# Layer 0's causal triangle as a 128-column matmul instead of GpSimd's selects

## The chip, the cores and the metric

The kernel runs on one core of a Trainium2 chip. The core has TensorE (PE, matmuls into PSUM), VectorE (DVE), ScalarE (ACT), GpSimd (POOL) and SyncE (SP, which issues most DMAs). The metric is the device time of one execution in microseconds, as the median of several runs.

## The reference, cut to what matters

Two pre-norm transformer layers follow one another: attention and a mixture of experts, then attention and a feed-forward with 4-bit weights. The change lies in the attention of layer 0, with 4 batches, 512 tokens, 16 heads of width 16 and a causal mask:

```
b, s, d = x.shape                                # 4, 512, 256
qkv = jnp.einsum('bsd,od->bso', x, w_project)    # reshaped to 3 x 16 heads x 16
att = jnp.einsum('bhqd,bhkd->bhqk', q, k) / math.sqrt(HEAD_DIM)
causal = jnp.triu(jnp.ones((s, s), dtype=bool), k=1)
att = jnp.where(causal[None, None, :, :], jnp.float32(-1000000000.0), att)
att = jax.nn.softmax(att, axis=-1)
out = jnp.einsum('bhqk,bhkd->bhqd', att, v)
...
x = x + _L0_attn_ref(_layernorm(x, axis=-1), L0_attn_w_project, L0_attn_w_out)
```

## The kernel before

Layer 0's attention takes a batch at a time (4 batches; the middle two are turns of a hardware loop), and in a batch four groups of four heads (`g` 0 to 3), so 16 groups in all. Each engine has its own program, written out by hand, and the engines meet at semaphores. One list (`in_group`) sets the order of a group's steps on PE, ACT and DVE alike.

A group has six **score units** (`ST_UNITS`, `score_unit`, line 661 on PE). A unit computes transposed scores, keys on partitions and queries on columns, for the key block `kt` (128 keys) and the queries from that block on. Units 0 and 1 are two heads each with 512 columns (`kt` 0), units 2 and 3 two heads each with 384 columns (`kt` 1), unit 4 four heads with 256 columns (`kt` 2), unit 5 four heads with 128 columns (`kt` 3). The row maximum has been folded into the matmul's rows, so that ACT can take the exponential right away (`exponentials`, line 766) and write `pt` in SBUF. The first 128 columns of each head are the diagonal block, in which half of the entries are to be zero. GpSimd zeroes them in `pt` with one select for each unit (line 530), and counts the semaphore `masked`. PE's **values** (`values`, line 675, four steps `kt` 0 to 3) multiply `pt` by `v`, and wait for `masked`. The scores lie in two pairs of PSUM banks, so unit u waits until ACT has read unit u-2.

Between these steps the list puts **work** for the next group or batch, in two further PSUM banks: the row maxima (`max_scores`, lines 582 and 586 on PE, reduced by DVE on line 857, ten items for each group), the turning of the maxima (line 609; DVE writes them as `mt_hi` and `mt_lo`, and SP copies these into the rows of `qs`), and in group 0 of each batch also the values of the batch (line 547), the transposed input of the next batch (lines 554, 725, 815), its queries and keys (lines 547, 730, 820), and the projection of the batch before (lines 594, 602, 853). A work item waits until DVE has read the item two places before. `max_scores` masks its own diagonal blocks already by a second matmul with `maskneg` (-3e38 above the diagonal) and the identity, accumulated onto the block (line 586). That is the pattern that the change uses.

GpSimd has other work in this stage: nine pieces for each batch (`split_next`, lines 482 to 499), which split a quarter of the next stage's weights after the DMA `w_next` has landed. Its program takes them between the selects: in batches 0 to 2 from group 1 on, behind every second unit; in the last batch behind every unit of groups 0 and 1.

Of the kernel before, what the change touches and what calls it, by code (L numbers as in the profile page):

```python
# [21 lines left out]
ALU = mybir.AluOpType  # L22
# [3 lines left out]
P = 128  # L26
# [22 lines left out]
def reach(eng, sem, value):  # L49

    if not (isinstance(value, int) and value <= 0):
        eng.wait_ge(sem, value)


def wait_alone(eng, sem, value, passed):

    eng.wait_ge(sem, value)
    eng.sem_inc(passed, 1)
# [3 lines left out]
def work_between(pieces):  # L62

    todo = iter(pieces)

    def some(k=1):
        for piece in islice(todo, k):
            piece()
    return some
# [100 lines left out]
def tie_break(e):  # L170

    return (4 - e) * STEP
# [88 lines left out]
def layer0_attention(nc, glob, A):  # L261
    X, ps, ident, identb = glob["X"], glob["ps"], glob["ident"], glob["identb"]
    passed_dve, passed_pool, passed_sp = glob["passed"]
    scratch_q, scratch_k = glob["scratch_q"], glob["scratch_k"]
    with ExitStack() as stack:
        st = Store(nc, stack)
# [8 lines left out]
        maskneg = st.sb("maskneg", [P, P], BF16)  # L275
# [11 lines left out]
        qs = st.sb("qs", [SHIFT + 2, H0, S], BF16)  # L287
        ks = st.sb("ks", [SHIFT + 2, H0, S], BF16)
# [5 lines left out]
        pt = [st.sb(f"pt{k}", [P, HG, S - P * k], F32) for k in range(G)]  # L294
# [26 lines left out]

        s_work, s_taken, s_mx = st.sem("bank_work"), st.sem("bank_taken"), st.sem("row_max")
        s_mthi, s_shift = st.sem("mthi"), st.sem("shift")
        s_st, s_exp, s_msk, s_pv = st.sem("scoreT"), st.sem("expd"), st.sem("masked"), st.sem("pv0")
        s_raw, s_den, s_rec, s_oT = st.sem("raw0"), st.sem("den0"), st.sem("rec0s"), st.sem("oT0")
        s_norm = st.sem("norm0")
        s_xr, s_xrlo, s_mag0, s_lg0, s_ties = (st.sem(n) for n in ("xr0", "xrlo0", "mag0", "lg0s", "ties_made"))
# [9 lines left out]
        ST_UNITS = [(0, (0, 1)), (0, (2, 3)), (1, (0, 1)), (1, (2, 3)), (2, (0, 1, 2, 3)), (3, (0, 1, 2, 3))]  # L337
# [18 lines left out]
        def all_batches(eng, batch):  # L356
            batch(0, True, False)
            with eng.Fori(1, B - 1) as b:
                batch(b, False, False)
            batch(B - 1, False, True)  # L360
# [11 lines left out]
        with nc.Block() as block:  # L372
# [86 lines left out]
            @block.gpsimd  # L459
            def _(pool):  # L460
                pool.memset(ones_row[:, :], 1.0).then_inc(const, 1)
                pool.memset(half[:, :], -0.5).then_inc(const, 1)
                pool.memset(maskneg[:, :], 0.0).then_inc(const, 1)

                pool.wait_ge(const, 3)

                pool.affine_select(out=maskneg[:, :], in_=maskneg[:, :], compare_op=ALU.is_ge, fill=NEG, base=0,
                                   pattern=[[-1, P]], channel_multiplier=1).then_inc(const, 1)

                def split_next(b):  # L470

                    def after(n, ins):
                        def piece():
                            if n is not None:
                                wait_alone(pool, s_next, NEXT * b + n, passed_pool)
                            ins().then_inc(s_next, 1)
                        return piece
                    r_hi, r_lo, e_hi, e_lo = (q[:, b] for q in quarters)

                    def first():  # L480
                        wait_alone(pool, load_next, 32 * b + 32, passed_pool)
                        pool.tensor_copy(r_hi, w_next[:, 0, :, :]).then_inc(s_next, 1)

                    def first_bias():
                        wait_alone(pool, load_b, 32 * b + 32, passed_pool)

                        if not (isinstance(b, int) and b == 0):
                            wait_alone(pool, s_b3, 96 * b, passed_pool)
                        pool.tensor_copy(b_part[:, 0, :], b_next[:, :]).then_inc(s_next, 1)
                    return [  # L490
                        first,
                        after(None, lambda: pool.tensor_copy(e_hi, w_next[:, 1, :, :])),
                        first_bias,
                        after(1, lambda: pool.tensor_tensor(r_lo, w_next[:, 0, :, :], r_hi.bitcast(F32), ALU.subtract)),
                        after(2, lambda: pool.tensor_tensor(e_lo, w_next[:, 1, :, :], e_hi, ALU.subtract)),
                        after(3, lambda: pool.tensor_tensor(b_next[:, :], b_next[:, :], b_part[:, 0, :], ALU.subtract)),
                        after(6, lambda: pool.tensor_copy(b_part[:, 1, :], b_next[:, :])),
                        after(7, lambda: pool.tensor_tensor(b_next[:, :], b_next[:, :], b_part[:, 1, :], ALU.subtract)),
                        after(8, lambda: pool.tensor_copy(b_part[:, 2, :], b_next[:, :])),
                    ]  # L500

                def root(b):

                    wait_alone(pool, s_mv, G * b + G, passed_pool)
                    pool.tensor_scalar(rstd[:, :], mv[:, :, 1], EPS, None, ALU.add).then_inc(s_rstd, 1)
                    wait_alone(pool, s_rstd, 2 * b + 1, passed_pool)
                    pool.tensor_tensor(rstd[:, :], rstd[:, :], half[:, :], ALU.pow).then_inc(s_rstd, 1)

                root(0)
                pool.wait_ge(s_rstd, 2)  # L510
                pool.memset(ones4[:, :], 0.0).then_inc(s_ties, 1)
                pool.wait_ge(s_ties, 1)
                pool.memset(ones4[0:4, :], 1.0).then_inc(s_ties, 1)
                pool.memset(glob["stage"][:, :, :], 0.0).then_inc(rows_set, 1)
                pool.wait_ge(rows_set, 1)
                for e in range(E):
                    pool.memset(glob["stage"][0:4, 0, D * e:D * (e + 1)], -e * ZERO_STEP).then_inc(rows_set, 1)

                def batch(b, first, last):
                    more = work_between(split_next(b))  # L520
                    root(b + 1)
                    if first:
                        for e in range(E):
                            pool.tensor_scalar(ties[:, e, :], identb[:, :], tie_break(e), None, ALU.mult).then_inc(s_ties, 1)
                    for g in range(NG):
                        for u, (kt, heads) in enumerate(ST_UNITS):

                            wait_alone(pool, s_exp, 6 * (NG * b + g) + u + 1, passed_pool)
                            t = pt[kt][:, heads[0]:heads[-1] + 1, 0:P]
                            pool.affine_select(out=t, in_=t, compare_op=ALU.is_ge, fill=0.0, base=0,  # L530
                                               pattern=[[0, len(heads)], [1, P]],
                                               channel_multiplier=-1).then_inc(s_msk, 1)
                            if last and g < 2 or g and u % 2:
                                more()

                all_batches(pool, batch)

            @block.tensor
            def _(pe):
# [111 lines left out]
                def score_unit(b, g, u):  # L651
                    kt, heads = ST_UNITS[u]
                    t = NG * b + g
                    if u == 0:
                        pe.wait_ge(s_shift, 32 * t + 32)

                    reach(pe, s_exp, 6 * t + u - 1)
                    for i, h in enumerate(heads):
                        c, w = st_col(u, i)
                        h += HG * g  # L660
                        mm = pe.matmul(ps[:, c:c + w], ks[:, h, P * kt:P * (kt + 1)], qs[:, h, P * kt:],  # L661
                                       start=True, stop=True, skip_group_check=True)
                    mm.then_inc(s_st, 1)

                def values(b, g, kt, values_taken):
                    t = NG * b + g
                    pe.wait_ge(s_msk, 6 * t + (2, 4, 5, 6)[kt])
                    if kt == 0:

                        reach(pe, s_raw, t)  # L670
                        if g == 0:

                            pe.wait_ge(s_taken, values_taken)
                    for h in range(HG):
                        mm = pe.matmul(ps[HB * h:HB * (h + 1), PVB * BANK + P * kt:(PVB + 1) * BANK],
                                       v[:, kt, HG * g + h, :], pt[kt][:, h, :],
                                       start=(kt == 0), stop=(kt == G - 1), skip_group_check=True)
                    mm.then_inc(s_pv, 1)
# [1397 lines left out]
def build(nc, A, out, phases=(1, 2, 3, 4)):  # L2076
    with ExitStack() as stack:
# [33 lines left out]
        if 1 in phases:  # L2111
            layer0_attention(nc, glob, A)
# [66 lines left out]
```

## Time and profile before

| what | value |
|---|---|
| time, median of 3 runs | 1227.91 us (1227.71 to 1230.26) |
| the profiled execution's own time | 1230.62 us |
| its span | 1228.9 us |
| TensorE busy | 1027.0 us, 84% |
| VectorE, ScalarE, GpSimd busy | 868.6, 499.1, 297.4 us |
| line 530 (GpSimd's selects) | 96 of them, 46.1 us |
| line 661 (score matmuls) | 256 of them |
| layer 0's attention on PE | score units from 49.99 us on, the last values at 286.50 us |

Busy times of different engines overlap, and their sum means nothing. A timeline row gives the start, the length, the engine, the line and the operation; xN says that N instructions of one kind are merged into it; the bracket names the idle time before the first of them and who ended it. A matmul's length holds its way through the array, so the cost of one in a row of several is the distance from its start to the next start. PEclk is the granted clock of TensorE as a share of full speed.

### The profile page before, as it was taken

How to read it: one execution, taken by the hardware profiler on the slowest of the kernel's cores; microseconds unless marked ns; L12 is line 12 of the kernel's file. 1: busy time of each engine (PE TensorE's matmuls, PEld its weight loads, DVE VectorE, ACT ScalarE, POOL GpSimd, SP SyncE). 2: the span in 40 equal slices, each digit the busy share in tenths (PEclk: the TensorE clock that was granted, in tenths of full speed). 3: DMA queues.
4: the chain of work that ended last, by engine and by line, in shares of the span. 5: the costliest groups of instructions: out<-in, count | busy, mean ns of one | idle time of the engine just before them, and what ended most of it. 6: DMA issues, size and time to landing. Idle time of an engine off the chain costs nothing. (4 is left out here: it accounts for less than half of the span.)

```text
span 1228.9 us, 20311 instructions
## 1 busy us (share of the span) xinstructions
PE 1027.0 (84%) x6960; PEld 591.5 (48%) x6960; DVE 868.6 (71%) x1556; ACT 499.1 (41%) x972; POOL 297.4 (24%) x337
## 2 busy tenths in 40 slices
PE   3798888798778788788398898988968799999997
PEld 1344444445444454443144474654746355656564
DVE  4677666643999999999867628448382577777775
ACT  2144444354465564655344314223130244444443
POOL 3233334440423324323111302203143410000000
PEclk9699999898899898897698898898968899999999
DMA  6622121201001010010000100000010100000000
GB/s 168 107 71 87 53 88 52 70 2 43 1 1 43 1 43 0 0 44 0 5 14 10 27 2 18 19 1 26 9 31 22 35 1 18 1 18 0 1 17 18
DMA packets 37082, 35.79 MB, mean 29 GB/s; under 512 B 8584, under 2 KB 33416, under 8 KB 37008
## 3 DMA queue, kind: packets, MB, share of 16 engines
q1 hardware_dynamic: 35728, 33.79, 9.6%
q10 hardware_dynamic: 1280, 1.05, 0.7%
q8 instruction: 42, 0.69, 0.2%
q14 instruction: 32, 0.26, 0.1%
HBM read 27.28 MB, written 6.29 MB: 27 GB/s over the span
## 5 line engine op out<-in xcount | busy, mean ns | idle before, releaser
L857 DVE TENSOR_REDUCE bm<-ps 128x4 f32<-128x512 f32 x160 | 106.3, 685 | 42.0 <-PE ps L586 31.9
L766 ACT ACTIVATE pt<-ps 128x1024 f32<-128x1024 f32 (+1 forms) x96 | 82.7, 881 | 84.3 <-PE ps L661 83.0
L1968 ACT ACTIVATE g<-ps 128x512 f32<-128x512 f32 x64 | 38.2, 597 | 133.0 <-PE ps L1917 133.0
L582 PE MATMUL ps<-ks,qs 96*128 96x512 bf16 (+3 forms) x256 | 71.6, 326 | 23.3 <-DVE bm L857 10.0
L2018 DVE SCALAR_TENSOR_TENSOR g<-g,ps 128x512 f32<-128x512 f32 x64 | 43.9, 685 | 62.6 <-ACT g L1968 62.3
L1726 DVE TENSOR_TENSOR qk_lo<-ps,qk_hi 128x512 bf16<-128x512 f32 x80 | 54.8, 684 | 42.9 <-ACT qk_hi L1618 36.5
L1495 PE MATMUL ps<-xT_hi,wq_hi 128*128 128x512 bf16 x160 | 68.6, 429 | 15.8 <-DVEq L1757 8.8
L155 POOL TENSOR_TENSOR mag_gu<-stage 128x512 f32<-128x512 fp8e4 x20 | 22.0, 1099 | 238.3 <-DVE stage L142 238.3
L1618 ACT ACTIVATE qk_hi<-ps 128x512 bf16<-128x512 f32 x80 | 47.8, 598 | 74.5 <-PE ps L1495 74.4
L1495 PE MATMUL ps<-wp_hi,oT_hi 128*128 128x256 bf16 x256 | 71.2, 278 | 4.9 <-DVE oT_lo L1719 4.9
L530 POOL TENSOR_SCALAR_AFFINE_SELECT pt<-pt 128x256 f32<-128x256 f32 (+1 forms) x96 | 46.1, 483 | 118.7 <-ACT pt L766 118.3
L1932 PE MATMUL ps<-ew_hi,it_hi 128*128 128x256 bf16 x256 | 69.8, 273 | 5.4 <-DVE it_lo L2034 5.4
L1495 PE MATMUL ps<-wp_lo,oT_hi 128*128 128x256 bf16 x256 | 71.0, 277 | 0.0
L1495 PE MATMUL ps<-wp_hi,oT_lo 128*128 128x256 bf16 x256 | 71.0, 277 | 0.0
L1932 PE MATMUL ps<-ew_lo,it_hi 128*128 128x256 bf16 x256 | 69.8, 273 | 0.0
L1932 PE MATMUL ps<-ew_hi,it_lo 128*128 128x256 bf16 x256 | 69.8, 273 | 0.0
L176 PE MATMUL ps<-stage,ones 128*128 128x512 bf16 x128 | 52.2, 408 | 20.3 <-DVE X L1287 8.2
L1495 PE MATMUL ps<-xT_lo,wq_hi 128*128 128x512 bf16 x160 | 68.0, 425 | 0.0
L1167 ACT ACTIVATE far<-far 128x256 f32<-128x256 f32 x128 | 51.3, 402 | 40.4 <-DVE far L1277 40.4
L1287 DVE SCALAR_TENSOR_TENSOR X<-ps,cw,X 128x256 f32<-128x256 f32 (+1 forms) x128 | 61.9, 483 | 8.2 <-DVE X L1287 4.9
L1495 PE MATMUL ps<-xT_hi,wq_lo 128*128 128x512 bf16 x160 | 67.0, 419 | 0.0
L1161 ACT ACTIVATE wt<-wt 128x2048 f32<-128x2048 f32 x16 | 30.6, 1915 | 87.6 <-POOL wt L1026 87.6
(254 smaller groups left out, 2816.1 us busy)
## 6 DMA issues: line engine op xcount, KB each, us to landing
qs<-scratch_q SPq DMA_DIRECT2D x64, 64.0 KB, 2.6
ks<-scratch_k SPq DMA_DIRECT2D x48, 64.0 KB, 2.5
q_next<-in_w_qkv SPq DMA_DIRECT2D x4, 768.0 KB, 4.6
X<-in_x SPq DMA_DIRECT2D x4, 512.0 KB, 7.0
w_next<-in_router_w SPq DMA_DIRECT2D x4, 512.0 KB, 4.1
w_next<-in_expert_w SPq DMA_DIRECT2D x4, 512.0 KB, 5.0
p_next<-in_w_proj SPq DMA_DIRECT2D x4, 512.0 KB, 5.5
out<-X SPq DMA_DIRECT2D x8, 256.0 KB, 2.3
```

The lines of the kernel that those rows point to most:

```text
L176: pe.matmul(out, ones4[:, :], bias, start=True, stop=False)
L530: pool.affine_select(out=t, in_=t, compare_op=ALU.is_ge, fill=0.0, base=0, pattern=[[0, len(heads)], [1, P]], channel_multiplier=-1).then_ ...
L582: pe.matmul(ps[:, o + P * i:o + P * (i + w)], qs[0:SHIFT, h, P * j:P * (j + 1)], ks[0:SHIFT, h, P * k0:P * (k0 + w)], start=(i == 0), stop ...
L766: act.activation(pt[kt][:, heads[0]:heads[-1] + 1, :], src, ACT.Exp).then_inc(s_exp, 1)
L857: ins = dve.tensor_reduce(bm[:, 2 * g + i // 5, 4 * (i % 5):4 * (i % 5) + 4], src.rearrange("p (k q) -> p k q", k=4), AX_X, ALU.max)
L1167: act.activation(far[:, e, :], far[:, e, :], ACT.Copy, accum_out=cw[t % 2][:, e:e + 1]).then_inc(s_cw, 1)
L1287: dve.scalar_tensor_tensor(x, bank(4 + u, D, D * e), c_t[:, 2 * u + e:2 * u + e + 1], x, ALU.mult, ALU.add).then_inc(s_c, 1)
L1495: mm = pe.matmul(out, lhs[a](c), rhs[b_](c), start=(n == 0), stop=(n == 3 * chunks - 1), **kw)
L1618: act.activation(qk_hi[:, m // (HQ + 1), m % (HQ + 1), :], bank(QK_BANK[m]), ACT.Copy).then_inc(s_qkhi, 1)
L1726: dve.tensor_tensor(qk_lo[:, k, h, :], bank(QK_BANK[m]), qk_hi[:, k, h, :], ALU.subtract).then_inc(s_qklo, 1)
L1932: mm = pe.matmul(bank(6 + t // 2, D, D * (t % 2)), a[m % 2][:, P * t:P * (t + 1)], w[2][:, m % 2, D * (m // 2):D * (m // 2 + 1)], start=(m ...
L2018: dve.scalar_tensor_tensor(g2[m % 2][:, :], g2[m % 2][:, :], 1.0, bank(2 * PAIR[m]), ALU.add, ALU.mult).then_inc(s_in, 1)
```

## The change

GpSimd's selects go. Behind each head's score matmul comes a second one with 128 columns: the stationary operand is `maskneg`, the moving one the identity, and so the transposed triangle of -3e38 is added to the diagonal block in PSUM. The exponential then gives zero there. The values wait for the exponentials (`expd`) in place of the selects (`masked`). GpSimd keeps its waits for the exponentials, which pace its nine pieces.

```
                     for g in range(NG):
-                        for u, (kt, heads) in enumerate(ST_UNITS):
+                        for u in range(len(ST_UNITS)):
                             wait_alone(pool, s_exp, 6 * (NG * b + g) + u + 1, passed_pool)
-                            t = pt[kt][:, heads[0]:heads[-1] + 1, 0:P]
-                            pool.affine_select(out=t, in_=t, compare_op=ALU.is_ge, fill=0.0, base=0,
-                                               pattern=[[0, len(heads)], [1, P]],
-                                               channel_multiplier=-1).then_inc(s_msk, 1)
                             if last and g < 2 or g and u % 2:
                                 more()
...
-                        mm = pe.matmul(ps[:, c:c + w], ks[:, h, P * kt:P * (kt + 1)], qs[:, h, P * kt:],
-                                       start=True, stop=True, skip_group_check=True)
+                        pe.matmul(ps[:, c:c + w], ks[:, h, P * kt:P * (kt + 1)], qs[:, h, P * kt:],
+                                  start=True, stop=False, skip_group_check=True)
+                        mm = pe.matmul(ps[:, c:c + P], maskneg[:, :], identb[:, :],
+                                       start=False, stop=True, skip_group_check=True)
                     mm.then_inc(s_st, 1)
...
                 def values(b, g, kt, values_taken):
                     t = NG * b + g
-                    pe.wait_ge(s_msk, 6 * t + (2, 4, 5, 6)[kt])
+                    pe.wait_ge(s_exp, 6 * t + (2, 4, 5, 6)[kt])
```

On PE, in the second half of a group, from the last heads of unit 4 to unit 5. Before (`qs,ks` are scores, `ks,qs` and `maskneg,identb` a row maximum, `pt,v` values):

```order
L661 MATMUL ps<-qs,ks 128x256 x3
L52 REGISTER_ALU
L582 MATMUL ps<-ks,qs 128x512 [waits bank_taken]
L586 MATMUL ps<-maskneg,identb 128x128
L667 REGISTER_ALU
L675 MATMUL ps<-pt,v 32x384 [waits masked]
L675 MATMUL ps<-pt,v 32x384 x3
L661 MATMUL ps<-qs,ks 128x128 [waits expd]
L661 MATMUL ps<-qs,ks 128x128 x3
```

And now, at the same place, where line 657 is the score matmul, 659 the new one, and 578, 582 and 673 are what 582, 586 and 675 were:

```order
L657 MATMUL ps<-qs,ks 128x256
L659 MATMUL ps<-identb,maskneg 128x128
L52 REGISTER_ALU
L578 MATMUL ps<-ks,qs 128x512 [waits bank_taken]
L582 MATMUL ps<-maskneg,identb 128x128
L665 REGISTER_ALU
L673 MATMUL ps<-pt,v 32x384 [waits expd]
L673 MATMUL ps<-pt,v 32x384 x3
L657 MATMUL ps<-qs,ks 128x128 [waits expd]
L659 MATMUL ps<-identb,maskneg 128x128
L657 MATMUL ps<-qs,ks 128x128
L659 MATMUL ps<-identb,maskneg 128x128
```

Every score matmul has a second one behind it, and the values wait for the exponential; the rest of PE's order stands.

On GpSimd, at the start of the last batch. Before:

```order
L505 TENSOR_SCALAR rstd<-mv 128x4 [waits mv0s]
L507 TENSOR_TENSOR rstd<-rstd,half 128x4 [waits rstd0s]
L530 AFFINE_SELECT pt<-pt 128x2x128 [waits expd]
L482 CAST rw_hi<-w_next 128x2x512 [waits load_next0]
L530 AFFINE_SELECT pt<-pt 128x2x128 [waits expd]
L492 CAST ew_hi<-w_next 128x2x512
L530 AFFINE_SELECT pt<-pt 128x2x128 [waits expd]
L489 CAST b_part<-b_next 2x512 [waits load_b0,b3]
```

And now:

```order
L505 TENSOR_SCALAR rstd<-mv 128x4 [waits mv0s]
L507 TENSOR_TENSOR rstd<-rstd,half 128x4 [waits rstd0s]
L482 CAST rw_hi<-w_next 128x2x512 [waits expd,load_next0]
L492 CAST ew_hi<-w_next 128x2x512 [waits expd]
L489 CAST b_part<-b_next 2x512 [waits expd,load_b0,b3]
L494 TENSOR_TENSOR rw_lo<-w_next,rw_hi 128x2x512 [waits expd,next0]
```

Before, the second select, for which PE's first values wait, stood behind a cast that waits for a DMA. Now nothing that PE's values wait for stands on GpSimd.

## Rows read from the trace of the kernel before

**Rows 1.** The page: TensorE's busy time, and its clock in 40 slices.

```profile
PE 1027.0 (84%) x6960; PEld 591.5 (48%) x6960; DVE 868.6 (71%) x1556; ACT 499.1 (41%) x972; POOL 297.4 (24%) x337
PEclk9699999898899898897698898898968899999999
```

**Rows 2.** PE's waits from 49.99 to 286.9: us in total, times, longest.

```profile
PE ps L582 <- DVE bm L857: 9.0, 12, 1.4
PE ps L554 <- DVE xn L807: 4.6, 3, 1.7
PE ps L675 <- POOL pt L530: 4.3, 3, 3.6
```

**Rows 3.** The score matmuls of line 661: count, and lengths in ns.

```profile
L661 PE MATMUL ps<-qs,ks x256: 219/323/634, 50.0 to 284.8; 98*128 98x512 bf16 x32, 98*128 98x384 bf16 x32, 98*128 98x256 bf16 x32, 98*128 98x128 bf16 x32
```

**Rows 4.** Timeline of PE in a regular group (group 3 of batch 0).

```profile
97.08 0.27 PE L609 MATMUL ps<-ident,mx 128*16 128x128 f32 x1
...
98.21 0.22 PE L586 MATMUL ps<-maskneg,identb 128*128 128x128 bf16 x1
98.27 0.22 PE L582 MATMUL ps<-ks,qs 96*128 96x128 bf16 x1
...
98.39 0.49 PE L661 MATMUL ps<-qs,ks 98*128 98x384 bf16 x2
...
99.63 0.22 PE L586 MATMUL ps<-maskneg,identb 128*128 128x128 bf16 x1
100.56 0.39 PE L582 MATMUL ps<-ks,qs 96*128 96x512 bf16 x1 [0.71 <-DVE bm L857]
```

**Rows 5.** Timeline of DVE in the same group.

```profile
97.39 0.28 DVE L831 TENSOR_SCALAR mt_hi<-ps 16x128 bf16<-16x128 f32 x1 [0.29 <-PE ps L609]
...
99.82 1.91 DVE L857 TENSOR_REDUCE bm<-ps 128x4 f32<-128x512 f32 x3
102.85 0.69 DVE L857 TENSOR_REDUCE bm<-ps 128x4 f32<-128x512 f32 x1 [1.12 <-PE ps L586]
```

**Rows 6.** Timeline of PE in group 0 of batch 1.

```profile
112.81 1.26 PE L554 MATMUL ps<-ident,xn 128*128 128x128 f32 x8 [1.44 <-DVE xn L807]
...
114.88 0.34 PE L582 MATMUL ps<-ks,qs 96*128 96x384 bf16 x1 [0.49 <-DVE xT_lo L815]
...
120.48 0.65 PE L594 MATMUL ps<-ident,o_norm 128*128 128x128 f32 x4 [1.01 <-DVE qk_lo L820]
...
123.68 1.06 PE L675 MATMUL ps<-pt,v 128*32 128x512 f32 x8
```

**Rows 7.** Timelines of PE and POOL in group 0 of batch 3.

```profile
238.59 0.28 PE L586 MATMUL ps<-maskneg,identb 128*128 128x128 bf16 x1
...
241.02 1.04 POOL L482 CAST rw_hi<-w_next 128x1024 fp32r<-128x1024 f32 x1 [8.76 <-DMA w_next<-in_expert_w]
...
242.47 1.94 PE L675 MATMUL ps<-pt,v 128*32 128x512 f32 x8 [3.60 <-POOL pt L530]
```

**Rows 8.** Stretches: us, busy (x) of PE, PEld, DVE, ACT, POOL; PEclk; DMA.

```profile
95.49:105.91 10.42, 9.51 (x89) 4.60 (x86) 8.02 (x19) 5.61 (x7) 5.63 (x10) 1.00 0.18 53
172.00:175.00 3.00, 1.56 (x10) 1.32 (x9) 2.12 (x6) 0.49 (x1) 0.00 (x0) 0.81 0.02 1
235.00:238.50 3.50, 3.17 (x15) 2.12 (x16) 2.59 (x6) 0.91 (x2) 0.00 (x0) 0.54 0.53 127
238.50:242.00 3.50, 0.37 (x2) 0.00 (x0) 0.69 (x1) 0.50 (x1) 0.98 (x1) 0.97 0.47 177
242.00:245.40 3.40, 2.93 (x14) 1.08 (x15) 0.00 (x0) 0.00 (x0) 3.40 (x7) 0.52 0.00 0
```

**Rows 9.** Timeline of PE in groups 2 and 3 of batch 3.

```profile
266.35 0.50 PE L661 MATMUL ps<-qs,ks 98*128 98x384 bf16 x2 [0.41 <-ACT pt L766]
...
270.74 1.11 PE L675 MATMUL ps<-pt,v 128*32 128x256 f32 x16 [0.36 <-POOL pt L530]
...
272.74 0.38 PE L176 MATMUL ps<-stage,ones 128*128 128x512 bf16 x1 [0.35 <-DMA stage<-b_part]
...
286.50 0.43 PE L675 MATMUL ps<-pt,v 128*32 128x128 f32 x8 [0.37 <-POOL pt L530]
```

More of the change, by code:

```diff
@@ L323, in layer0_attention @@
         s_mthi, s_shift = st.sem("mthi"), st.sem("shift")
-        s_st, s_exp, s_msk, s_pv = st.sem("scoreT"), st.sem("expd"), st.sem("masked"), st.sem("pv0")
+        s_st, s_exp, s_pv = st.sem("scoreT"), st.sem("expd"), st.sem("pv0")
         s_raw, s_den, s_rec, s_oT = st.sem("raw0"), st.sem("den0"), st.sem("rec0s"), st.sem("oT0")
```

## The prediction, made before the result was known

> **What bounds the kernel now.** I read the page first: TensorE is busy for 84% of the span, and its clock stands near full in most slices [rows 1]. The chain that ended last runs through TensorE too, but it begins far behind layer 0's attention, so it doesn't say what sets the pace there. For that I took PE's waits from the first score unit to the last values [rows 2]: in 237 us the longest totals are 9.0 us for DVE's reductions, 4.6 us for the normalised input and 4.3 us for GpSimd's selects. The stage is mostly TensorE's own work, and the selects hold its matmuls up on three occasions only, of which one is 3.6 us long; elsewhere they are ready in time. Then I read one regular group instruction by instruction [rows 4, 5], then a group 0 [rows 6], and the last batch [rows 7, 9]. Behind this stage the program is unchanged, and it starts only when the last values are through, so what the stage gains or loses goes straight into the time.
>
> **What one added matmul costs.** There are as many as score matmuls, 256 [rows 3]. The trace has the same operation already: line 586, 128 columns in bf16 with 128 rows, and its neighbour of line 582 with 128 columns. From the start of the one at 98.21 to the score matmul at 98.39 there are three such matmuls in a row, 0.18 us, so 0.060 each; at the rows' rounding I take 0.058 us at the full clock and 0.116 at half. The weight loads hide there, and stationary operands of 96 and 128 rows alternate just as they will now with 98 and 128 rows [rows 4]. Bounds: nothing, where PE would have waited anyway; and 0.060 for all 256, which is 15.4 us.
>
> The Trainium skill ("TensorE: Matmul & The Clock Gate", section "Back-to-back issue gap") says that in a stream of pairs of weight load and matmul the spacing with 128 columns is about 81 ns, since both take part. The row says 60 ns in just such a stream, and the trace decides; by the page the 190 matmuls that count below would cost 15.4 us in place of 11.1, and the sum would be 4.3 us higher, an estimate by that page.
>
> **Which of them lie on the path.** A regular group (group 1 to 3 of batches 0 to 2, group 1 of batch 3: ten) lasts 10.42 us [rows 8].
> - Units 0 and 1 (4 added) stand ahead of line 609 at 97.08. DVE has been idle for 0.29 us when that ends, and it is then busy without a break until 101.73, so PE's delay becomes DVE's: on the path.
> - Units 2 and 3 (4 added) stand in the stretch in which PE waits for DVE: PE has issued everything by 99.69 and starts again only at 100.56, when DVE's first reduction of the three from 99.82 is through. 4 x 0.058 = 0.23 us fits into those 0.87 us: hidden.
> - Units 4 and 5 (8 added) come behind 100.56, where PE runs without a wait and DVE waits for PE (1.12 us at 102.85): on the path.
>
> So 12 of 16 count: 10 x 12 x 0.058 = +7.0 us [rows 4, 5]. ACT stays ahead: it is busy for 5.6 of the 10.42 us [rows 8].
>
> Group 0 of batches 1 and 2: again all but unit 2's two, which vanish in the 0.49 us wait at 114.88. Unit 3's stand inside the matmuls of queries and keys, and the chain from PE by ACT and DVE back to 120.48 carries them on. 2 x 14 x 0.058 = +1.6 us [rows 6]. Group 0 of batch 0: unit 0 at half clock (the page's second slice is at 0.6 [rows 1]), 2 x 0.116, units 4 and 5 at full, 8 x 0.058; unit 1 hides behind a copy on DVE, units 2 and 3 behind the transposed input as above: +0.7. Group 0 of batch 3: units 0, 1, 4, 5, 12 x 0.058 = +0.7; units 2 and 3 in waits for DVE. Groups 2 and 3 of batch 3: 2 + 8 in each; the rest stands where PE waits for ACT's exponentials (0.41 at 266.35 [rows 9]): 20 x 0.058 = +1.2. Together 190 matmuls count, +11.1 us with the roundings (7.0 + 1.6 + 0.7 + 0.7 + 1.2 = 11.2).
>
> **What goes away.** Two short waits of the values for a select, 0.36 and 0.37 us, whose exponentials are finished by then: -0.7 us [rows 9]. And the long one. In the last batch GpSimd's first cast waits 8.76 us for the DMA `w_next`, the second select stands behind it, and PE, done at about 238.87, gets its values only at 242.47: 3.60 us idle [rows 7]. The exponentials that these values need were written long before. After the change they start at once: -3.6 us. GpSimd still waits for that DMA, but its nine pieces have the time until the router's matmuls at 272.74 us [rows 9], 31 us behind the landing, and GpSimd has nothing else to do there. The clock comes on top. While PE is idle (0.37 us busy in 238.5 to 242) it is granted 0.97, and for the 3.4 us after that 0.52, the lower of its two levels: the eight matmuls of these values take 1.94 us there, and 1.06 us in batch 1 [rows 6, 7, 8]. Before the idle time PE had been busy for 3.17 of 3.5 us, and the clock had just come back from 0.54 to full. Without the idle time I expect it to stay: of the 2.9 us from 242.47 to 245.4 half goes, -1.4 us. Bounds of this: 0 and -1.5.
>
> DVE, ACT and GpSimd lose nothing: 96 selects leave GpSimd (46 us busy), which nobody waits for elsewhere. The second exponential of the masked entries costs what any entry does. What is late next once the selects are gone is the exponential of unit 5: in a regular group it ends ahead of the last values, and both move together.
>
> **The sum.** +11.2 - 0.7 - 3.6 - 1.4 = +5.5 us; with the unrounded terms 5.4. The profiled execution's own time is 1230.62 us, so a like one would come to 1236.0. The median of the runs shown is 2.7 us lower, at 1227.91, so I expect a median of **1233.3 us**. What a measurement of this kernel can tell from no change is about 0.2%, 2.5 us either way; the runs shown spread by as much, 1227.71 to 1230.26.
>
> **The rivals.**
> 1. *The masks fill PE's waits (faster).* Place: the waits for DVE, 9.0 us in twelve, and for the input, 4.6 [rows 2]. If all 256 went into such waits only the gains would be left: -5.7 us, 1222.2. If only the regular groups' did: 5.4 - 7.0 = -1.6 us, 1226.3. It decides at line 609: if DVE were still busy when the turned maxima arrive, PE's delay there would be free. For it: PE waits 0.71 us in each regular group. Against: the wait is over before units 4 and 5, and DVE is the one that waits around them [rows 4, 5].
> 2. *Nothing is hidden, or each costs more.* 256 x 0.060 = 15.4, less 5.7: +9.7 us, 1237.6. For it: work is put in between, and PE's sequencer has more to issue. Against: the 0.87 us before 100.56 are plainly idle [rows 4].
> 3. *The clock repays more.* PE falls to half also where it waits for the normalised input: 1.56 us busy in 3 us, and then about 3 us at the low level [rows 8]. In batch 1 the same wait had no such fall. There are two falls of this sort, in batches 2 and 3, each worth at most 1.7 us; if both stayed away: 5.4 - 3 = +2.4 us, 1230.3. Against: the added matmuls don't shorten that wait.
> 4. *The stall stays in another shape*, say because the DMA's landing holds up something else of the last batch: 5.4 + 5.0 = +10.4 us, 1238.3. Against: nothing but GpSimd reads `w_next`, and PE's only other wait on its results is the router's.
>
> **How the numbers follow.** Forecast 0.60, rival 1 0.12 (of it 0.07 as the full one), rival 2 0.10, rival 3 0.13, rival 4 0.05. The forecast's own range is 1230.5 to 1236: the stall's clock share may not come back (+1.4), the clock in the rest of the program falls where it will (its runs spread 2.5 us). Faster by over 0.2% means under 1225.5: the full rival 1 and part of the half one, 0.11. Slower by over 0.2% means above 1230.4: the forecast, rivals 2 and 4, and about a third of rival 3, with a little of the forecast lost below: 0.73. Within: 0.16. The range that should hold it 8 times in 10: 1227.5 to 1239.
>
> **What would show it.** Regular groups of 11.1 us in place of 10.42, and PE's wait before the first values down to about 0.5 us; starts 0.06 us apart in unit 5; no wait of the values for anything in the last batch, and PE at full clock from 238.5 on; GpSimd's first cast still waiting for the DMA, with PE at work beside it; the last values at about 292 us in place of 286.5. Regular groups of 10.4 us would prove rival 1, of 11.4 rival 2. The forecast is wrong if a group grows by less than 0.5 us, or if PE still stands still around 240 us.

## The result, and the profile after

The changed kernel takes 1236.08 us (median of 5 runs, 1234.55 to 1236.85) against 1227.91 us before (5 runs, 1227.25 to 1232.93), a ratio of 1.0056 with a 95% interval of 1.0034 to 1.0077: by this ratio 6.9 us slower, between 4.2 and 9.5 (the two medians lie 8.2 us apart). Forecast were 5.4 us more and 1233.3, with 1230.5 to 1236 as the forecast's own range, at whose upper edge the median lies. The time alone doesn't tell the forecast from rival 2 (1237.6); the groups in the trace do. The sign, the price and place of the masks and the end of the stall were as forecast; what TensorE's clock would do was not.

The page after: the lines that answer to [rows 1], and GpSimd's.

```profile
PE 1032.0 (84%) x7142; PEld 604.9 (49%) x7216; DVE 868.6 (70%) x1556; ACT 500.0 (40%) x972; POOL 253.0 (20%) x241
PEclk9699999999899798897799798898978899999999
```

GpSimd is rid of the 96 selects and 44 us of work, and nothing is faster for it: it was waited for in a few places only. PE's waits after, from the first score unit to the last values, in us in total, times, longest, answer to [rows 2]:

```profile
PE ps L578 <- DVE bm L855: 9.1, 12, 1.2
PE ps L550 <- DVE xn L805: 4.5, 3, 1.7
PE ps L590 <- DVE qk_lo L818: 2.3, 2, 1.1
```

Lines 578, 550 and 855 are the old 582, 554 and 857. The waits for DVE's reductions and for the input are as they were, within 0.1 us, and GpSimd's row is gone. So the stall went, and neither of the two large waits took up the new matmuls.

**A regular group** (group 3 of batch 0). PE's timeline after, against [rows 4]; line 657 is the old 661, line 659 the new matmul, 605 the old 609:

```profile
98.12 0.39 PE L657 MATMUL ps<-qs,ks 98*128 98x512 bf16 x1
98.34 0.22 PE L659 MATMUL ps<-identb,maskneg 128*128 128x128 bf16 x1
98.40 0.38 PE L657 MATMUL ps<-qs,ks 98*128 98x512 bf16 x1
...
99.95 0.27 PE L605 MATMUL ps<-ident,mx 128*16 128x128 f32 x1
...
100.73 0.22 PE L659 MATMUL ps<-identb,maskneg 128*128 128x128 bf16 x1
100.91 0.34 PE L578 MATMUL ps<-ks,qs 96*128 96x384 bf16 x1
...
102.50 0.22 PE L582 MATMUL ps<-maskneg,identb 128*128 128x128 bf16 x1
103.43 0.39 PE L578 MATMUL ps<-ks,qs 96*128 96x512 bf16 x1 [0.71 <-DVE bm L855]
...
106.65 0.23 PE L657 MATMUL ps<-qs,ks 98*128 98x128 bf16 x1
106.71 0.22 PE L659 MATMUL ps<-identb,maskneg 128*128 128x128 bf16 x1
106.77 0.22 PE L657 MATMUL ps<-qs,ks 98*128 98x128 bf16 x1
```

A mask takes 0.06 us wherever PE isn't waiting: 98.34 to 98.40, 106.71 to 106.77. The lengths (0.22) overlap; only the starts tell the price. The surprise is in the bracket at 103.43: still 0.71 us. The masks of units 2 and 3 did vanish, but in two smaller gaps ahead of it, which stand in PE's timeline of before, same columns:

```profile
97.47 0.49 PE L661 MATMUL ps<-qs,ks 98*128 98x384 bf16 x2
98.04 0.34 PE L582 MATMUL ps<-ks,qs 96*128 96x384 bf16 x1
...
99.00 0.22 PE L586 MATMUL ps<-maskneg,identb 128*128 128x128 bf16 x1
99.34 0.28 PE L582 MATMUL ps<-ks,qs 96*128 96x256 bf16 x1
```

Two 384-column matmuls take 0.33 us and a 128-column one 0.06, so PE stood still for 0.24 us ahead of 98.04 and 0.28 ahead of 99.34. In the changed kernel the same gaps are 0.12 (100.73 to 100.91, less 0.06) and 0.16 us: less by 0.12 each, which is two masks. DVE's timeline of the same group answers to [rows 5]:

```profile
100.26 0.28 DVE L829 TENSOR_SCALAR mt_hi<-ps 16x128 bf16<-16x128 f32 x1 [0.41 <-PE ps L605]
...
102.69 1.91 DVE L855 TENSOR_REDUCE bm<-ps 128x4 f32<-128x512 f32 x3
105.97 0.69 DVE L855 TENSOR_REDUCE bm<-ps 128x4 f32<-128x512 f32 x1 [1.36 <-PE ps L582]
```

Counted from each group's first score matmul, `mt_hi` comes at 2.14 us (before 1.90), the last reduction at 7.85 (7.36) and the end at 11.14 (10.42). PE's delay reaches DVE in full: 0.24 us from units 0 and 1, as much again by the last reduction, the rest behind it.

**Groups 0.** PE's timeline after in batch 1, where it had no stretch at the low clock before [rows 6]:

```profile
116.40 1.25 PE L550 MATMUL ps<-ident,xn 128*128 128x128 f32 x8 [1.44 <-DVE xn L805]
...
118.47 0.50 PE L578 MATMUL ps<-ks,qs 96*128 96x384 bf16 x1 [0.37 <-DVE xT_lo L813]
...
119.87 0.63 PE L543 MATMUL ps<-xT_lo,first_lg 128*128 128x512 bf16 x1 [0.58 <-DVEq L861]
120.30 1.06 PE L543 MATMUL ps<-xT_hi,first_lg 128*128 128x512 bf16 x2
...
125.34 0.65 PE L590 MATMUL ps<-ident,o_norm 128*128 128x128 f32 x4 [1.13 <-DVE qk_lo L818]
```

512-column matmuls start 0.43 us apart (119.87 to 120.30) where the full clock gives 0.22 (98.12 to 98.34): the lower level. The masks are not needed for that. In e3 below, which has none and PE's program as before, PE fell at the same place behind the same two waits as in [rows 6], and that group 0 of batch 1 took 31.66 us against 28.99:

```profile
113.77 1.25 PE L554 MATMUL ps<-ident,xn 128*128 128x128 f32 x8 [1.44 <-DVE xn L807]
...
115.84 0.50 PE L582 MATMUL ps<-ks,qs 96*128 96x384 bf16 x1 [0.49 <-DVE xT_lo L815]
...
117.24 0.63 PE L547 MATMUL ps<-xT_lo,first_lg 128*128 128x512 bf16 x1 [0.58 <-DVEq L863]
117.66 1.06 PE L547 MATMUL ps<-xT_hi,first_lg 128*128 128x512 bf16 x2
```

PE's and GpSimd's timelines after at the start of the last batch answer to [rows 7]:

```profile
248.54 1.08 PE L590 MATMUL ps<-ident,o_norm 128*128 128x128 f32 x4 [0.71 <-DVE o_norm L885]
...
249.85 0.31 PE L582 MATMUL ps<-maskneg,identb 128*128 128x128 bf16 x1
250.09 1.77 PE L673 MATMUL ps<-pt,v 128*32 128x512 f32 x8
```

```profile
251.36 1.04 POOL L482 CAST rw_hi<-w_next 128x1024 fp32r<-128x1024 f32 x1 [8.30 <-DMA w_next<-in_expert_w]
```

The cast waits as before, and PE's values no longer wait with it. But they start at the low clock, 1.77 us for work that takes 1.06 at full [rows 6].

Stretches after, with the columns of [rows 8]: a regular group; group 0 of batches 1, 2 and 3; the low stretch around the first values of the last batch; and what lies between the last values and the next stage.

```profile
98.12:109.26 11.14, 10.43 (x105) 5.61 (x101) 8.01 (x19) 5.78 (x7) 2.41 (x4) 1.00 0.17 50
109.26:140.25 30.99, 25.80 (x184) 15.15 (x182) 17.50 (x41) 10.37 (x15) 1.26 (x2) 0.94 0.30 99
174.07:205.08 31.01, 25.81 (x184) 15.16 (x182) 17.48 (x41) 10.37 (x15) 1.27 (x2) 0.94 0.30 98
238.92:260.56 21.64, 19.21 (x153) 12.35 (x149) 13.20 (x34) 6.97 (x9) 9.34 (x8) 0.92 0.23 69
247.60:251.20 3.60, 2.89 (x18) 1.20 (x14) 2.05 (x5) 1.33 (x2) 0.00 (x0) 0.58 0.78 270
295.16:305.07 9.91, 5.84 (x37) 4.44 (x38) 2.07 (x4) 2.54 (x6) 0.11 (x1) 1.00 0.00 0
```

The last of these in the trace of before, same columns:

```profile
286.50:299.20 12.70, 8.80 (x38) 6.45 (x38) 2.07 (x4) 2.36 (x5) 0.11 (x1) 0.73 0.00 1
```

That stretch holds the last output projection. It took 12.7 us at a mean clock of 0.73 in this execution of before, and 9.8 us at full clock in two further executions of the same kernel (below). It is why the two profiled times, 1236.70 and 1230.62, differ by 6.1 us only, though the attention stretch, from the first score matmul to the last values, grew from 236.5 to 245.6.

### The profile page after: what moved, and what is told of

Its sections match the earlier page's. It is cut to its first block and busy times, and to the rows that moved or that the text cites. A ratio compares the mean times of both kernels' runs of the same rounds, so it can differ in the third digit from the quotient of the medians.

```text
span 1234.9 us, 20653 instructions
## 1 busy us (share of the span) xinstructions
PE 1032.0 (84%) x7142; PEld 604.9 (49%) x7216; DVE 868.6 (70%) x1556; ACT 500.0 (40%) x972; POOL 253.0 (20%) x241
## 5 line engine op out<-in xcount | busy, mean ns | idle before, releaser
L178 PE MATMUL ps<-rw_hi,xr_hi 128*128 128x512 f32 x128 | 65.9, 515 | 6.9 <-issue 4.2
L1493 PE MATMUL ps<-xT_hi,wq_hi 128*128 128x512 bf16 x144 | 60.5, 420 | 1.7 <-DVE qk_lo L1724 1.4
L657 PE MATMUL ps<-qs,ks 98*128 98x512 bf16 (+3 forms) x256 | 61.5, 305 | 0.3 <-ACT pt L764 0.3
```

Of the source, the lines that this page charges most:

```text
L178: pe.matmul(out, x_hi(c), w_hi[:, c, cols], start=False, stop=False)
L1493: mm = pe.matmul(out, lhs[a](c), rhs[b_](c), start=(n == 0), stop=(n == 3 * chunks - 1), **kw)
```

## The experiments

Each times against its own runs of before on the same chip. "Stretch" is that attention stretch in the profiled execution: 236.5, 238.3 and 236.3 us in three profiles of before, 245.6 and 244.7 in two of after.

**e4, the changed kernel once more** (no edit), and e9 and e10, the kernel before once more (no edit), for the spread from execution to execution.

> The kernel after, unchanged, for a second profile and more times on the same chip. The first profile showed half-clock stretches behind the wait for the normalised input in batches 0, 1, 2 and 3; the kernel before in batches 2 and 3 only. Theory A (these falls come and go from one execution to the next): this profile has a different set of them, and the time is within 0.3% of the first, 1233 to 1237 us. Rival (the added matmuls make PE fall there each time): the same four again.

> The kernel before, unchanged, for a second profile. The first one showed the last batch's group 0 at 25.56 us with half clock at 235.0 and 241.8, and half clock for 6.8 us over the last projection (289.6), and its time, 1230.6, was 2 to 3 us above its median. If the time of an execution is moved by where these stretches fall, this profile has another set, and the regular groups (10.42 us) and the 3.6 us wait for the selects are the same; groups 0 of batches 1 and 2 between 29.0 and 31.7 us. If the stretches belong to the kernel, the same set again.

> The same once more: a third profile of the kernel before, with the same two readings.

e4 took 1234.87 us (5 runs), ratio 1.0047 [1.0034, 1.0060]. e9 and e10 were profiled once each, at 1229.3 and 1227.1. Their longest values' waits for a select were 3.4 and 3.3 us, so the stall is no accident of one execution. Means of the profiles: stretch 237.0 before, 245.1 after, +8.1. On the low stretches in the groups 0 the expectations are answered so: e4 shows the same four again as after, against its first theory; e9 has one more than the first profile of before (in batch 0), and its batch 2 took 30.27 us in place of 29.41; e10 has the first profile's set, though its last projection ran at the full clock.

**e1, nobody masks**, and **e2, both mask**. e1 is the changed kernel without line 659's matmuls; e2 the kernel before with them, its selects kept.

```
e1:  -  mm = pe.matmul(ps[:, c:c + P], maskneg, identb, start=False, stop=True)
e2:  before, and behind each score matmul of line 661
     +  mm = pe.matmul(ps[:, c:c + P], maskneg, identb, start=False, stop=True)
```

> The kernel after without the 256 new matmuls: nobody masks, so the output is not the reference's. It is the removal of GpSimd's selects alone. Theory A (the forecast's terms: the selects held PE up for 3.6 + 0.7 us, and the half clock behind the long wait for 1.4): 5.7 us under the kernel before, ratio 0.995, and no wait of the values for another engine around the last batch's w_next DMA. Theory B (the gain is smaller, because PE's clock falls elsewhere instead or the next wait takes over): 2 us or less under before, ratio 0.998 to 1.000.

> The kernel before with the 256 new matmuls added and the selects kept (they find the zeros already there). It is the price of the matmuls alone. Theory A: 190 on the path at 0.058 us: +11.1 us, ratio 1.009, regular groups of 11.15 us, and the wait around 240 us is still there. Rival (each costs more than its spacing, through ACT or the clock): +14 us or more, ratio 1.0115 up.

e1: 1223.23 us (6 runs), ratio 0.9945 [0.9928, 0.9963], -6.8 us. e2: 1243.16 (4 runs), ratio 1.0108 [1.0094, 1.0123], +13.3. The halves add up: 13.3 - 6.8 = +6.5, and the change measured 6.9. The masks cost 13.3 where the sum had 11.2, and taking the selects off the path repaid 6.8 where it had 5.7. The intervals are wide, though (11.6 to 15.1 and 4.5 to 8.9): e2's time lies between its theory (+11.1) and its rival (+14), and only its regular groups, 11.14 us long, show that a mask costs no more than its spacing there. The profiled execution of e1 is its slowest (1227.39; the fastest took 1219.79). Its stretch is 233.4 us, 3.7 below before, but that is a sum of unlike things: group 0 of the last batch is 3.4 us shorter than the mean of before, the other places 2.6 together, and group 0 of batch 1, with a long low stretch and no mask in it, 2.3 us longer. What the faster executions of e1 had no profile shows. e2 keeps the stall, shortened by PE's coming later; its PE timeline:

```profile
253.69 1.94 PE L677 MATMUL ps<-pt,v 128*32 128x512 f32 x8 [2.62 <-POOL pt L530]
```

**e5, e6, e7, masks of two units only** (units 0 and 1; 2 and 3; 4 and 5), the other units unmasked.

```
+  masked = u in (0, 1)      # (2, 3) in e6, (4, 5) in e7
+  if masked: mm = pe.matmul(ps[:, c:c + P], maskneg, identb, ...)
```

> The kernel after with the new matmuls in units 0 and 1 only (64 of 256); the other units are not masked. Read from the lengths of the ten regular groups in the profile, which are 10.42 us in the kernel without any new matmul and 11.15 with all. Theory A (accounting by place: units 0 and 1 stand ahead of the turned maxima and count in full): 10.42 + 4 x 0.06 = 10.66 us. Rival (the cost is spread over all 16 alike, 0.73 / 16 each): 10.60 us.

> The same with the new matmuls in units 2 and 3 only (64 of 256). Theory A: they vanish in PE's wait for DVE, so the regular groups stay at 10.42 us and PE's wait ahead of the first values stays 0.71 us long or a little shorter. Rival (all alike): 10.60 us.

> The same with the new matmuls in units 4 and 5 only (128 of 256). Theory A: all count, 10.42 + 8 x 0.06 = 10.90 us. Rival (all alike): 10.79 us. Beside it, where the half-clock stretches of the four groups 0 lie: in three profiles with all 256 they stood behind the wait for the normalised input in every batch, in four profiles without any in one to three of them. If that is a matter of where the batch's period puts the wait, this kernel, whose period lies between, has another set; if the new matmuls as such bring the fall, they are there in all four again.

One run each: 1230.0, 1223.2 and 1229.4 us. The times of single runs say little where 15 runs of before on that chip lie between 1227.53 and 1232.96; group 2 of batch 0, from start to start in PE's timeline, says it cleanly. e5, then e6, then e7:

```profile
86.10 0.39 PE L658 MATMUL ps<-qs,ks 98*128 98x512 bf16 x1
...
96.77 0.39 PE L658 MATMUL ps<-qs,ks 98*128 98x512 bf16 x1
```

```profile
85.81 0.60 PE L658 MATMUL ps<-qs,ks 98*128 98x512 bf16 x2
...
96.23 0.61 PE L658 MATMUL ps<-qs,ks 98*128 98x512 bf16 x2
```

```profile
86.25 0.61 PE L658 MATMUL ps<-qs,ks 98*128 98x512 bf16 x2
...
97.15 0.61 PE L658 MATMUL ps<-qs,ks 98*128 98x512 bf16 x2
```

10.67, 10.42 and 10.90 us, against 10.42 before: +0.24 (this group 0.25, its neighbours 10.66 and 10.67), 0 and +0.48. That is 4, 0 and 8 masks of 0.06, and together the 0.72 of the full change. Which masks hide and which don't is settled for the regular groups.

These three also bear on the clock. e7's low stretches stand in batches 0, 1 and 3, so in another set, as the first reading of its expectation had it. In e6 the last batch's group 0 has none: 19.81 us at a granted clock of 1.00, and 1.07 us for the first values. Its stretch, columns of [rows 8]:

```profile
228.18:247.99 19.81, 17.17 (x141) 11.14 (x138) 13.11 (x34) 6.89 (x9) 9.36 (x8) 1.00 0.24 75
```

**e3, the stall alone taken away.** The kernel before, but in group 0 of the last batch GpSimd's pieces of the next weights (`more()`, which holds the cast that waits for the DMA) begin behind the fourth select, not the first.

```
-  if last and g < 2 or g and u % 2:
+  if last and (g == 1 or g == 0 and u > 2) or g and u % 2:
```

> The kernel before, selects kept and no new matmul; only in the last batch GpSimd begins its nine pieces behind unit 3 of group 0 in place of unit 0, so that the wait for w_next no longer stands ahead of the selects for the first values. Theory A: it gets the 3.6 + 1.4 us of the stall: 5.0 us under before, ratio 0.996, PE busy through 238 to 242 us. Rival (the stall only moves to the second values, or the split weights come late for the router at 272 us): ratio 0.998 to 1.002. If A holds, it is faster than both kernels.

1227.66 us (12 runs), ratio 0.9982 [0.9969, 0.9995]: -2.2 us, less than the 3.6 of the stall. Group 0 of the last batch fell from 25.56 to 19.81 us, but group 1 rose from 10.43 to 12.11. GpSimd's timeline, then PE's:

```profile
256.13 2.13 POOL L495 TENSOR_TENSOR ew_lo<-w_next,ew_hi 128x1024 bf16<-128x1024 f32 x1
258.21 0.41 POOL L530 TENSOR_SCALAR_AFFINE_SELECT pt<-pt 128x256 f32<-128x256 f32 x1
```

```profile
260.14 0.85 PE L675 MATMUL ps<-pt,v 128*32 128x384 f32 x8 [1.57 <-POOL pt L530]
```

The pieces pushed into group 1 stand before its selects, and PE waits 1.57 us there. The stall was moved in part, as the rival of the expectation said. In the profiled execution, at 1230.22 us as slow as any of the twelve, group 0 of batch 1 was also 2.7 us longer, the low stretch shown above.

**e8 and e11, the pieces where nobody waits.** The kernel before, with the pieces behind units 4 and 5 of group 0 and 3 to 5 of group 1 of the last batch:

```
-  if last and g < 2 or g and u % 2: more()
+  if last:
+      more({(0, 4): 1, (0, 5): 4, (1, 3): 1, (1, 4): 1, (1, 5): 2}.get((g, u), 0))
+  elif g and u % 2: more()
```

> The kernel before, with its selects, and GpSimd's nine pieces of the last batch placed so that no select that PE is about to need has one ahead: one behind unit 4 and four behind unit 5 of group 0, then behind units 3, 4, 5 of group 1. Theory A: the wait at 240 us is gone as with the pieces begun at unit 3, and the 1.57 us wait that this made in group 1 is gone too; groups 0 and 1 of the last batch together come down from 36.0 to about 30.5 us, and the time to 3.5 to 5.5 us under the kernel before, ratio 0.9955 to 0.997. Rival (what the stall costs is given back by the clock or by the DMA that the router waits for): ratio 0.998 or more.

> The kernel with the selects and the nine pieces spread, once more. In its first profile the last batch's groups 0 and 1 took 5.5 us less than in the first profile of before, but its median was only 2.1 us lower. If the first profile of before was an execution with an unlucky clock, the ratio stays at 0.9966 to 0.9987 and the last batch's group 0 of before's other profiles is 24.0 to 25.6 us; if the gain of 5 us is real on the average, the ratio comes out at 0.996.

e8: 1226.47 us (11 runs), ratio 0.9976 [0.9966, 0.9987]. e11, the same code again: 1225.59 (12 runs), ratio 0.9967 [0.9954, 0.9980]. So 2.9 to 4.1 us below before, and some 10 below the changed kernel, with the selects kept. This version beats both, by little, but in both measurements the whole interval lies below 1. Of the expected 3.5 to 5.5 us e8 showed 2.9, and e11 came out at the better end of its first reading. That reading's reason, an unlucky first profile of before, doesn't hold: group 0 of the last batch took 25.5 and 25.3 us in the other two as well. The last batch of e8: groups 0 and 1 (stretches, columns of [rows 8]), then PE's first values there.

```profile
228.35:248.16 19.81, 16.92 (x137) 10.80 (x134) 13.11 (x34) 6.88 (x9) 9.57 (x13) 1.00 0.26 74
248.16:258.81 10.65, 9.59 (x89) 4.65 (x85) 8.57 (x20) 5.58 (x7) 6.37 (x10) 1.00 0.01 2
```

```profile
238.63 1.06 PE L677 MATMUL ps<-pt,v 128*32 128x512 f32 x8
```

Groups 0 and 1 take 30.5 us together, as expected. Group 0 is 5.7 us shorter than the 25.5 of before. That is the stall and the low clock on both sides of it [rows 8]: no wait, a granted clock of 1.00, and 1.06 us for the values where e1 and the changed kernel need 1.93 and 1.77. The stretch is 232.4 us in e8 and 232.5 in e11; in both profiles the last projection then ran at the low clock (12.7 us), which hid up to 2.9 us of it.

## Why the prediction came out as it did

Measured are the differences between the mean profiles of before (three) and after (two).

| term | predicted | measured |
|---|---|---|
| ten regular groups | +7.0 | +7.1 |
| group 0 of batch 0 | +0.7 | +1.0 |
| groups 0 of batches 1 and 2 | +1.6 | +3.2 |
| group 0 of batch 3 (masks, stall, clock) | -4.3 | -3.8 |
| groups 2 and 3 of batch 3 (masks, short waits) | +0.5 | +0.6 |
| sum | +5.5 | +8.1 |

The regular groups grew by 0.71 to 0.73 us each, but group 3 of batch 1 by 0.59: it took 10.65 us in every profile with selects and without masks, and 10.52 in those without either, a small cost of the selects that the sum didn't have.

- *The price of a mask*, 0.058 us, held to a hundredth, and so did the count of 12 in 16 for regular groups (e5 to e7). The Trainium skill ("TensorE: Matmul & The Clock Gate", section "Back-to-back issue gap") puts such pairs at about 81 ns with 128 columns; at that a regular group would have grown by 0.97 us, an estimate by that page, and it grew by 0.72.
- *PE's wait before its first values would shrink to 0.5 us*: wrong as a thing to look for, right in the price. It stayed at 0.71, and the masks went into smaller waits ahead of it.
- *The stall*: gone, as forecast; it was 3.6, 3.4 and 3.3 us in the three profiles of before. That GpSimd's cast would still wait and PE work beside it is in the rows.
- *"Without the idle time I expect it to stay"*, said of the full clock, worth -1.4: as a statement on the clock this step failed. The forecast wanted the full clock from 238.5 us on; after shows a clock of 0.58 over 247.6 to 251.2, on the same work, and e1 without the stall takes 1.93 us for its first values. The clock had fallen not only after PE's idling but also before it (0.54 in [rows 8]); without the stall the low stretch lay on the values instead of partly on idle time. That full clock is possible there without the stall is shown by e3, e6, e8 and e11, whose group 0 took 19.8 us; e1, e5, e7 and both profiles of after had a low stretch, 21.6 to 22.3 us. In time the step lost little, and that is partly luck. An estimate: before, group 0 lay 5.6 us above those 19.8, of which 3.4 are the wait and 2.2 the clock; after, 1.8 above, of which 0.7 are masks and 1.1 the clock. So 1.1 us of clock came back in place of 1.4, because the low clock lay on both sides of the wait and the sum had counted only the side behind it.
- *The same term, where I had set nothing*: group 0 of batch 1 ran at full clock in three profiles of before and has a low stretch in both profiles of after (and in e2); batch 2 had one in all, and it now costs more. In batch 1 the 14 masks would make 29.0 + 0.8 = 29.8 us at full clock; measured are 31.0 and 30.9. Over both groups 1.6 us are missing, most of the gap between 5.5 and 8.1. Whether the masks brought it about is not shown: without any mask group 0 of batch 1 took 31.3 (e1) and 31.7 us (e3), and batch 2 took 30.3 (e9). What such a stretch costs differs with its place and length: 0.4 us in batch 2 before (29.4 against the 29.0 of batch 1) and 1.3 in batch 2 of e9, 1.2 in batch 1 after, where 512-column matmuls stand in it, and 2.7 in batch 1 of e3.
- *The last values* came at 295.16 us, where about 292 was forecast: the same clock terms.
- *The rivals.* 1, masks in PE's waits: out, groups grew by 0.72. 2, nothing hidden: out, e6. Its half "each costs more" is out too; a mask costs its 0.06 us at full clock, and what is above that lies in the groups 0. 3, the clock repays more: the wrong sign, the groups 0 of batches 1 and 2 became longer by 1.6 us more than their masks. 4, the stall in another shape: out for this change, but e3 has something like it, a wait for a select one group later.

The time of the runs, +6.9, lies below the +8.1 of the stretch. The last projection, at low clock in one of three profiles of before and in none of two after, makes up 0.9 us of the difference on the mean. That the sum came within 1.5 us of the measured 6.9 is luck in part: 2.6 us were missing from the stretch, and the projection hid some of them.

**Open:** whether the masks bring the low stretches about or merely shift the work under them. With all masks there was one in each of the four groups 0 in three of three profiles, with units 0 and 1 masked in all four as well, with units 4 and 5 masked in batches 0, 1 and 3, with units 2 and 3 masked only in batch 0, and without masks, in seven profiles of four programs, in two or three of the four groups, not always the same. Batch 1 had one in two of those seven (e1 and e3). So masks are not necessary for it; whether they make it likelier is open, for that is too few profiles, and the full clock in the last projection is as unexplained.

## What to carry to other kernels

Work that an idle engine does beside the pace-setting one is free until something blocks its queue; look what stands in front of it in program order (here a cast waiting 8.8 us for a DMA) before moving it onto the engine that sets the pace. Here 256 tiny matmuls cost 13 us to cure a stall of 3.6 that a changed place for nine conversion pieces cures without adding an instruction. Price an added matmul by the distance of starts, count only those outside a wait, and never book a clock gain as certain.

## What the runs showed of the hardware

- In group 0 of batch 1 PE ran at full clock behind waits of 1.44 and 0.49 us [rows 6], fell to the lower level behind waits of 1.44 and 0.37 us with masks between them, and fell in e3 behind the same 1.44 and 0.49 us without a mask. So the waits just ahead don't settle it. The low stretches also move between executions of one kernel: of before, batch 0 had one in one profile of three, the same output projection took 9.8 or 12.7 us, and the profiled stretch 236.3 to 238.3. One profile is not enough to book a term of 1 to 3 us.
- A select waits behind whatever was issued ahead of it on GpSimd. With the cast that waits for the DMA that was 3.3 to 3.6 us of PE's time, and behind a subtraction of 2.13 us (e3) it was 1.57.
